# Softmax attention on one core: two maxima for one pass, by a Relu of key differences on ScalarE, and 64-row products in pairs

## The chip, the cores and the metric

The kernel runs on one core of one Trainium2 chip. The metric is the device time of one execution in microseconds; the runs of the kernel before have a median of 1805.18 us. The engines are named as in the profile: PE is TensorE, PEld its weight loads, DVE is VectorE, ACT is ScalarE, POOL is GpSimd, SP is the engine that issues most transfers.

## The reference

The kernel computes a small language-model tower: an embedding, a softmax attention, a layer of experts, a second attention with Relu features, and a second layer of experts. The change lies in the first attention and in the embedding stage that prepares it. Four sequences of 1024 tokens have 12 heads of 16 features each:

```python
qkv = jnp.einsum('bnhd,hde->bnhe', xh, W_qkv) + b_qkv
q, k, v = jnp.split(qkv, 3, axis=-1)
scores = jnp.einsum('bihd,bjhd->bhij', q, k) / scale
p = jax.nn.softmax(scores, axis=-1)
attn = jnp.einsum('bhij,bjhd->bihd', p, v)
```

## The kernel before, in words

**Parts and stacks.** Queries and keys are split into three bf16 parts (high, middle, low). A stack puts six products of parts above each other in 96 partitions (`Q_STACK`, `K_STACK`, lines 43 to 45), so that one bf16 matmul of 96 rows gives an almost exact f32 product. Row 96 of the query stack holds minus the maximum of each query, row 96 of the key stack ones, so that a matmul of 97 rows gives scores with the maximum taken off.

**Embedding** (`embed_and_project`, lines 161 to 373). Eight chunks of 512 tokens run through a two-deep pipeline. POOL gathers rows of the table three chunks ahead (line 211) and makes the low parts by three subtractions per chunk (line 217). SP waits for them (line 229) and sends the parts to memory in four transfers per chunk (line 235). ACT writes `full` and the high parts (lines 320, 321) after the sends of two chunks before (line 319); at the end it loads the stacks of batch 0, group 0 (line 331). The stage ends with all engines meeting (line 164 in the profile).

**Attention** (`softmax_attention`, lines 376 to 723). The heads stand in three groups of four (`NG`, `GH`). For each of four batches and three groups there are 16 steps (two halves of 512 queries, eight tiles of 128 keys). A step issues, in PE's order of line 694: scores of the next step for heads 0 and 1 (`scores`, line 647), one maximum product, scores for heads 2 and 3, two maximum products, the products of this step's probabilities with V (`times_v`, line 679), one more maximum product. ACT takes exponentials of two heads at a time (`exps`, line 610) out of four PSUM banks; PE waits for ACT before it writes these banks again (line 645).

**Maxima.** A group needs 64 maximum units: four heads, eight query tiles, two halves of the keys (`max_units`, line 426). PE writes a unit to one of three PSUM slots in turn (`produce`, lines 651 to 668), DVE reduces it (`consume`, line 553) and so frees the slot (`ring_free`). The units of the next group are made five steps ahead (`AHEAD`, line 430); before the loop, all 64 units of group 0 and 20 of group 1 are made alone (`before`, line 432). I call this the lead-in. At the end of a group DVE combines the halves (line 573), PE transposes the maxima, and SP sends them through memory into row 96 (`load_max`, lines 472 to 477). SP also loads each group's stacks for the next batch, in 12 transfers, once the group's scores are done (lines 502 to 505). The batch loop is a hardware loop over three batches, with the last batch written out behind it (`turns`, line 462).

Lines that the prediction names: 319 (ACT's wait for sends), 622 (ACT's copy of the output, once per eight steps).

## Time and profile before

| | us |
|---|---|
| median of 3 runs (lowest to highest) | 1805.18 (1803.73 to 1810.18) |
| the profiled execution's own time | 1795.51 |
| its span, first to last instruction | 1793.9 |
| embedding stage, to the meeting of the engines | 0 to 109 |
| lead-in, maxima only | 110 to 161 |
| loop of 192 steps | 161 to 732 |
| all later stages | 732 to 1794 |

The page gives the busy time of each engine in the span (PE 1596.3, DVE 1090.1, ACT 627.6, POOL 423.1 us), then the span in 40 slices of 44.8 us with a digit for each engine's busy tenths, then groups of instructions by line. Durations of PE's products include their way through the array, so products that follow each other overlap in the records; their pitch is read from start to start. An idle time in brackets belongs to the engine just before the instruction and names what ended it.

### The profile page before, as it was taken

To read this page: it belongs to the slowest core of one execution; us is meant where nothing else is said; L and a number is where in the kernel's file an instruction comes from. 1 tells how busy PE (TensorE), PEld (TensorE's weight loads), DVE (VectorE), ACT (ScalarE), POOL (GpSimd) and SP (SyncE) were. 2 spreads that over 40 slices of the span, in tenths; PEclk is the share of its full clock that TensorE was granted. 3 is DMA by queue.
4 is the path that set the end of the run, shared out by engine and by line. 5 is a ranking of instruction groups with operands and counts; after the bars stand their busy time and mean duration, and the time that the engine had idled before them with its cause. 6 is when DMAs were issued, how large, how long until landed. Compare 5 with 4: busy or idle time off the path is not lost. (4 is left out here: it accounts for less than half of the span.)

```text
span 1793.9 us, 28354 instructions
## 1 busy us (share of the span) xinstructions
PE 1596.3 (89%) x8964; PEld 865.2 (48%) x8965; DVE 1090.1 (61%) x2478; ACT 627.6 (35%) x849; POOL 423.1 (24%) x518
## 2 busy tenths in 40 slices
PE   4779999999899999875999947899988989999997
PEld 2422332233233332574566634567775656666664
DVE  5978997899799893356233335565544943333336
ACT  3412666576566668410211102222123112212111
POOL 6650000000000000100455525000000226666650
PEclk9866999999999999885899977999899889999999
DMA  2470222022222200630211112000001401111116
GB/s 78 151 169 1 37 37 36 1 35 35 36 35 36 36 1 1 154 119 16 60 42 39 39 46 64 1 10 19 10 18 51 126 18 51 53 50 53 46 42 216
DMA packets 64847, 92.82 MB, mean 52 GB/s; under 512 B 9905, under 2 KB 50036, under 8 KB 63732
## 3 DMA queue, kind: packets, MB, share of 16 engines
q1 hardware_dynamic: 51520, 65.08, 15.3%
q0 software_dynamic: 12288, 25.18, 4.9%
q10 hardware_dynamic: 960, 1.57, 0.4%
q8 instruction: 41, 0.67, 0.2%
q14 instruction: 38, 0.31, 0.1%
HBM read 61.82 MB, written 29.98 MB: 51 GB/s over the span
## 5 line engine op out<-in xcount | busy, mean ns | idle before, releaser
L553 DVE TENSOR_REDUCE sa_half_max<-psum 128x1 f32<-128x512 f32 x768 | 494.5, 687 | 68.8 <-PE psum L656 50.0
L610 ACT ACTIVATE sa_probs<-psum 128x1024 f32<-128x1024 f32 x384 | 372.3, 1022 | 167.2 <-PE psum L647 165.7
L656 PE MATMUL psum<-k_stack,q_stack 96*128 96x512 bf16 x768 | 285.5, 410 | 19.7 <-DVE sa_half_max L553 9.6
L647 PE MATMUL psum<-q_stack,k_stack 97*128 97x512 bf16 x768 | 231.1, 385 | 6.3 <-ACT sa_probs L610 5.4
L656 PEld LDWEIGHTS psum<-k_stack,q_stack 96*128 96x128 bf16 x768 | 75.0, 98 | 274.7 <-issue 133.2
L679 PE MATMUL psum<-sa_probs,sa_v_ext 128*32 128x512 f32 x1536 | 206.6, 610 | 0.6 <-ACT sa_probs L610 0.6
L1580 PE MATMUL psum<-w_e_up_a,ex_xt 128*128 x448 | 172.5, 528 | 0.0
L1430 ACT ACTIVATE ex_silu<-psum 128x384 f32<-128x384 f32 (+1 forms) x112 | 59.3, 529 | 290.8 <-PE psum L1580 288.3
L1470 DVE COPY ex_to_rows<-slot_rows 128x2 uint32 (+1 forms) x56 | 12.8, 229 | 211.5 <-DMA y_rows<-ex_y,ex_to_rows 117.4
L1596 PE MATMUL psum<-w_e_down,ex_g_t 128*128 x752 | 137.2, 334 | 0.5 <-DVE ex_g_t L1462 0.5
L1596 PEld LDWEIGHTS psum<-w_e_down,ex_g_t 128*128 128x128 f32 x752 | 120.7, 190 | 34.5 <-issue 34.5
L1364 POOL DMA_INDIRECT y_rows<-ex_y,ex_to_rows x112 | 110.7, 988 | 98.7 <-DVE ex_y L1471 70.5
L1455 DVE TENSOR_TENSOR ex_g<-ex_silu,psum 128x384 f32<-128x384 f32 (+1 forms) x112 | 67.0, 602 | 96.6 <-PE psum L1580 85.1
L1333 POOL DMA_INDIRECT ex_x<-x_tokens,ex_tokens x112 | 110.6, 988 | 55.6 <-POOL ex_tokens L1339 39.5
L542 POOL COPY sa_v_ext<-v_nat 128x512 f32 x12 | 7.2, 613 | 474.4 <-PE psum L679 474.0
L647 PEld LDWEIGHTS psum<-q_stack,k_stack 97*128 97x128 bf16 x768 | 72.7, 99 | 88.6 <-ACT sa_probs L610 28.8
L1580 PEld LDWEIGHTS psum<-w_e_up_a,ex_xt 128*128 128x128 f32 x448 | 84.3, 192 | 60.6 <-issue 32.1
L1573 PE MATMUL psum<-ex_w_b,ex_xt 64*128 64x384 f32 (+1 forms) x448 | 98.9, 560 | 6.5 <-ACT ex_xt L1424 3.2
L1108 POOL TENSOR_TENSOR sh_work<-sh_work 128x512 f32<-128x512 f32 x6 | 8.9, 1480 | 307.1 <-ACT sh_work L1167 305.3
L1424 ACT COPY ex_xt<-psum 128x512 f32<-128x512 f32 x56 | 32.8, 586 | 127.0 <-PE psum L1562 127.0
L1462 DVE COPY ex_g_t<-psum 128x384 f32<-128x384 f32 (+1 forms) x112 | 63.7, 605 | 15.1 <-PE psum L1587 12.6
L679 PEld LDWEIGHTS psum<-sa_probs,sa_v_ext 128*32 128x32 f32 x1536 | 30.3, 108 | 81.3 <-issue 75.1
(286 smaller groups left out, 2183.1 us busy)
## 6 DMA issues: line engine op xcount, KB each, us to landing
attn<-y_rows SPq DMA_DIRECT2D x24, 384.0 KB, 4.6
q_stack<-qk_parts SPq DMA_DIRECT2D x66, 128.0 KB, 4.3
k_stack<-qk_parts SPq DMA_DIRECT2D x66, 128.0 KB, 6.6
qk_parts<-qk_split SPq DMA_DIRECT2D x16, 384.0 KB, 3.5
x_tokens<-x SPq DMA_DIRECT2D x16, 384.0 KB, 2.6
qk_parts<-qk_split SPq DMA_DIRECT2D x16, 192.0 KB, 4.4
w_e_down<-e_down SPq DMA_DIRECT2D x1, 3072.0 KB, 32.6
out<-h SPq DMA_DIRECT2D x8, 384.0 KB, 4.0
```

Of the source, the lines that this page charges most:

```text
L553: nc.vector.tensor_reduce(half_max[:, g, hd, qt, half:half + 1], slot, AX.X, ALU.max).then_inc(ring_free[r], 1)
L610: nc.scalar.activation(probs[:, st % 2, 2 * pair:2 * pair + 2, :], ps[:, 2 * pair:2 * pair + 2, :], ACT.Exp, scale=SCALE0).then_inc(exp_do ...
L647: last = nc.tensor.matmul(ps[:, hd, :], kst[:, g, hd, kt * P:(kt + 1) * P], qst[:, g, hd, half * HALF:(half + 1) * HALF], start=True, stop ...
L656: last = nc.tensor.matmul(ps[:, 4 + r, :], qst[0:SK, g, hd, qt * P:(qt + 1) * P], kst[0:SK, g, hd, half * 512:(half + 1) * 512], start=Tru ...
L679: last = nc.tensor.matmul(ps[hd * W:(hd + 1) * W, OUT, :], v_ext[:, g, kt, hd, :], probs[:, st % 2, hd, :], start=(kt == 0), stop=(kt == T ...
L1333: pool.indirect_dma_start(out=x[:, u, :], out_offset=None, in_=x_tokens, in_offset=bass.IndirectOffsetOnAxis(ap=tokens[:, u:u + 1], axis=0 ...
L1364: pool.indirect_dma_start(out=y_rows, out_offset=bass.IndirectOffsetOnAxis(ap=to_rows[:, u:u + 1], axis=0), in_=y[:, u, :], in_offset=None ...
L1455: nc.vector.tensor_tensor(g[:, u, :], silu[:, u, :], ps[:, PS_UP + u, 0:F], ALU.mult).then_inc(g_done, 1)
L1462: nc.vector.tensor_copy(g_t[:, u, :], ps[:, PS_G + u, 0:F]).then_inc(g_t_done, 1)
L1573: last = nc.tensor.matmul(ps[:, bank + u, 0:F], xt[rows_of, u, v, :], w_b[rows_of, u, :], start=True, stop=False)
L1580: nc.tensor.matmul(ps[:, bank + u, 0:F], xt[:, u, v, :], w.up(u, v), start=False, stop=True).then_inc(done, 1)
L1596: last = nc.tensor.matmul(ps[:, PS_Y, u * D:(u + 1) * D], g_t[:, u, c * P:(c + 1) * P], w.down(u, c), start=(c == 0), stop=(c == FC - 1))
```

## The change

Each group of units in a step becomes: a difference product for an even head, a product of an odd head with the first half of the keys, a "both" product for the even head, a product of the odd head with the second half. The keys of an even head are taken in pairs (j and j + 256 of a chunk). The difference product gives q(near key) - q(far key); ACT writes its Relu to SBUF; the "both" product gives q(far key), and one DVE instruction adds the two and takes the maximum. All maximum products use only the first four parts, 64 rows: rows 0 to 63 for even heads, rows 64 to 127 for odd heads, whose stacks are laid out anew (four parts in rows 64 to 127, two in rows 0 to 31, the maximum in row 32, zeros up to row 63), so that their scores now use 128 rows. The differences of keys are made by POOL in the embedding stage and sent and loaded like the parts. The loads of batch 0, group 0 move from ACT's end to SP, between the sends.

```diff
+SENDS = 6
+MAX_ODD = SK - DB
+def max_rows_of(odd):
+    return slice(DB, P) if odd else slice(0, DB)
+def score_rows_of(odd):
+    return slice(0, P) if odd else slice(0, SK + 1)
+def load_stack(eng, s, b, g, which, odd):
+    stack, order = ((s.q_stack, Q_STACK), (s.k_stack, K_STACK))[which]
+    for k, part in enumerate(order):
+        row = (DB + k * HD) % P if odd else k * HD
...
+        eng.dma_start(stack[row:row + HD, g, odd::2, :], src[odd]).then_inc(s.loaded[g], 16)
+def load_differences(eng, s, b, g):
+    for k, part in enumerate(K_STACK[:DB // HD]):
...
+        eng.dma_start(s.d_stack[k * HD:(k + 1) * HD, g, :, :], src[0]).then_inc(s.loaded[g], 16)
+STACK_LOADS = 4 * len(Q_STACK) + DB // HD
@@ embed_and_project, POOL
+            def take_apart(u, k, link):
+                pool.wait_ge(two["sent"][u], START + 16 * SENDS * k)
+                near, far = full[:, u, 1:3, 0:CHUNK // 2], full[:, u, 1:3, CHUNK // 2:CHUNK]
+                high, middle = (differences[:, u, :, part, :] for part in range(2))
+                link(nc.gpsimd.tensor_tensor(apart[:], near, far, ALU.subtract))
+                link(nc.gpsimd.tensor_copy(high, apart[:]))
+                nc.gpsimd.tensor_tensor(middle, apart[:], high, ALU.subtract).then_inc(two["apart"][u], 1)
+                pool.wait_ge(two["apart"][u], START + k + 1)
...
+                if chunk >= 0:
+                    take_apart(u, k, Chain(pool, m["ep_apart_link"], 2, chunk))
@@ embed_and_project, SP
-            with sp.Fori(0, B) as b:
+            for b in range(B):
                 for u in range(2):
                     sp.wait_ge(two["low"][u], START + 3 * (b + 1))
+                    sp.wait_ge(two["apart"][u], START + b + 1)
...
+                    for r, (src, row) in enumerate(((slice(0, P), 0), (slice(DB, P), P))):
...
+                        sp.dma_start(dst.rearrange("c r t -> r c t"), differences[src, u, r]).then_inc(two["sent"][u], 16)
+                    early = 2 * b + u - 3
...
+                    if 0 <= early < 4:
+                        load_stack(sp, s, 0, 0, early // 2, early % 2)
+                    if early == 3:
+                        load_differences(sp, s, 0, 0)
@@ embed_and_project, ACT
-                    act.wait_ge(two["sent"][u], START + 64 * k)
+                    act.wait_ge(two["sent"][u], START + 16 * SENDS * k)
+                    act.wait_ge(two["apart"][u], START + k)
...
-                load_stacks(act, s, 0, 0)
@@ softmax_attention
         def max_units(g, first, last):
-            return [("max", g, k // (2 * TB), k // 2 % TB, k % 2) for k in range(first, last)]
+            units = []
+            for k in range(first, last):
+                odd, half, qt, hd = k % 2, k // 2 % 2, k // 4 % TB, k // (4 * TB) * 2
+                units.append(("max", g, hd + 1, qt, half) if odd else
+                             ("both" if half else "difference", g, hd, qt, half))
+            return units
@@ load_max
+            for odd, row in enumerate((SK, MAX_ODD)):
+                sp.dma_start(qst[row:row + 1, g, odd::2, :], rows[odd]).then_inc(max_loaded[g], 16)
@@ POOL
+            nc.gpsimd.memset(qst[MAX_ODD:DB, :, 1::2, :], 0.0).then_inc(v_init, 1)
+            nc.gpsimd.memset(kst[MAX_ODD:DB, :, 1::2, :], 0.0).then_inc(v_init, 1)
@@ DVE, consume
+                if kind == "difference":
+                    return
                 slot = ps[:, 4 + r, :]
                 dve.wait_ge(ring_full[r], START + k + 1)
+                if kind == "both":
+                    hd, qt, _ = unit[2:]
+                    r_near, k_near = near
+                    dve.wait_ge(ring_free[r_near], START + k_near + 1)
+                    dve.nop(nofuse=True)
+                    nc.vector.tensor_tensor_reduce(ahead_of[:, u], slot, ahead_of[:, u], 1.0, LOWEST, ALU.add, ALU.max,
+                                                   half_max[:, g, hd, qt, 0:1]).then_inc(ring_free[r], 1)
@@ ACT
+            def ahead(r, k, u, r_taken, k_taken):
+                act.wait_ge(ring_full[r], START + k + 1)
+                act.wait_ge(ring_free[r_taken], START + k_taken + 1)
+                nc.scalar.activation(ahead_of[:, u], ps[:, 4 + r, :], ACT.Relu).then_inc(ring_free[r], 1)
...
                         exps(b, g, st)
+                        for unit in step_units(g, st, last)[0]:
+                            if unit[0] == "difference":
+                                ahead_in_turn(b, place[last][unit], last)
@@ PE
-                    last = nc.tensor.matmul(ps[:, hd, :], kst[:, g, hd, kt * P:(kt + 1) * P],
-                                            qst[:, g, hd, half * HALF:(half + 1) * HALF], start=True, stop=True)
+                    rows = score_rows_of(hd % 2)
+                    last = nc.tensor.matmul(ps[:, hd, :], kst[rows, g, hd, kt * P:(kt + 1) * P],
+                                            qst[rows, g, hd, half * HALF:(half + 1) * HALF], start=True, stop=True)
...
+                if kind in ("difference", "both"):
+                    rows = max_rows_of(0)
+                    slot, keys = ps[:, 4 + r, :], s.d_stack[rows, g, hd // 2, :]
+                    if kind == "both":
...
+                    last = nc.tensor.matmul(slot, qst[rows, g, hd, qt * P:(qt + 1) * P], keys, start=True, stop=True)
...
-            ORDER = ("scores", "maxima", "scores", "maxima", "maxima", "outputs", "maxima")
+            ORDER = ("scores", "maxima", "scores", "maxima", "outputs")
...
+                                for unit in left[:2]:
+                                    produce(b, unit, *uses(b, n))
+                                    n += 1
+                                left = left[2:]
```

## Rows read from the trace of the kernel before

**Rows 1.** The page's slices: busy tenths of PE and DVE in 40 slices.

```profile
PE   4779999999899999875999947899988989999997
DVE  5978997899799893356233335565544943333336
```

**Rows 2.** Stretches: us, busy PE, PEld, DVE, ACT, POOL (count), clock, DMA, GB/s.

```profile
110.00:160.60 50.60, 49.08 (x86) 8.74 (x85) 49.67 (x85) 0.00 (x0) 16.93 (x18) 0.50 0.36 77
170.00:300.00 130.00, 129.61 (x742) 40.52 (x740) 119.43 (x198) 90.04 (x95) 1.23 (x2) 1.00 0.18 26
692.00:731.00 39.00, 37.77 (x224) 8.05 (x222) 1.84 (x6) 35.22 (x38) 0.00 (x0) 1.00 0.01 1
```

**Rows 3.** Timeline of one loop step: start, length in us, engine, line.

```profile
171.71 0.39 PE L656 MATMUL psum<-k_stack,q_stack 96*128 96x512 bf16 x1
...
171.93 0.60 PE L647 MATMUL psum<-q_stack,k_stack 97*128 97x512 bf16 x2
172.13 2.59 DVE L553 TENSOR_REDUCE sa_half_max<-psum 128x1 f32<-128x512 f32 x4 [0.24 <-PE psum L656]
...
172.65 1.94 ACT L610 ACTIVATE sa_probs<-psum 128x1024 f32<-128x1024 f32 x2 [0.90 <-PE psum L647]
...
173.02 0.60 PE L656 MATMUL psum<-k_stack,q_stack 96*128 96x512 bf16 x2
...
173.54 1.07 PE L679 MATMUL psum<-sa_probs,sa_v_ext 128*32 128x512 f32 x8
...
174.54 0.39 PE L656 MATMUL psum<-k_stack,q_stack 96*128 96x512 bf16 x1
```

**Rows 4.** Timeline of PE in the expert stage, 64-row products among full ones.

```profile
962.16 1.99 PE L1573 MATMUL psum<-ex_w_b,ex_xt 64*128 64x512 f32 x8
964.08 2.87 PE L1596 MATMUL psum<-w_e_down,ex_g_t 128*128 x16
966.78 3.60 PE L1580 MATMUL psum<-w_e_up_a,ex_xt 128*128 x8
970.22 0.60 PE L1562 MATMUL psum<-ident,ex_x 128*128 128x128 f32 x4
```

**Rows 5.** Line 622, all of its instructions: ns min/median/max, first and last start.

```profile
L622 ACT COPY sa_out_t<-psum x24: 586/586/592, 189.0 to 732.4; 128x512 f32<-128x512 f32 x24
```

**Rows 6.** Timeline where the batch loop jumps back.

```profile
306.77 1.28 ACT L610 ACT_TABLE_LOAD   x1
...
308.07 3.77 ACT L610 ACTIVATE sa_probs<-psum 128x1024 f32<-128x1024 f32 x4
309.15 0.61 PE L647 MATMUL psum<-q_stack,k_stack 97*128 97x512 bf16 x2 [1.62 <-ACT sa_probs L610]
...
316.03 2.48 DVE L553 TENSOR_REDUCE sa_half_max<-psum 128x1 f32<-128x512 f32 x4 [7.64 <-issue]
316.78 0.61 PE L656 MATMUL psum<-k_stack,q_stack 96*128 96x512 bf16 x1 [4.69 <-DVE sa_half_max L553]
```

**Rows 7.** DVE: the lead-in's first reductions, all reductions, and a product of two tensors.

```profile
110.17 15.03 DVE L553 TENSOR_REDUCE sa_half_max<-psum 128x1 f32<-128x512 f32 x25 [5.92 <-PE psum L656]
...
L553 DVE TENSOR_REDUCE sa_half_max<-psum x768: 670/691/697, 110.2 to 687.6; 128x1 f32<-128x512 f32 x192
...
L1455 DVE TENSOR_TENSOR ex_g<-ex_silu,psum 128x512 f32<-128x512 f32 x40 | 27.5, 688 | 51.9 <-PE psum L1580 48.7 <-ACT ex_silu L1430 1.9
```

**Rows 8.** POOL's subtractions around one chunk, and SP at the embedding's end.

```profile
64.45 1.15 POOL L217 TENSOR_TENSOR qk_split<-ep_rest,qk_split 128x512 bf16<-128x512 f32 x1 [0.36 <-DVE qk_split L268]
...
72.90 1.53 POOL L217 TENSOR_TENSOR qk_split<-ep_rest,qk_split 128x512 bf16<-128x512 f32 x1 [1.10 <-DVE qk_split L268]
74.79 1.15 POOL L217 TENSOR_TENSOR qk_split<-ep_rest,qk_split 128x512 bf16<-128x512 f32 x1 [0.36 <-DVE qk_split L268]
...
105.65 2.72 SPq L235 DMA_DIRECT2D qk_parts<-qk_split  x4
109.01 2.91 SPq L157 DMA_DIRECT2D q_stack<-qk_parts  x6
```

More of the change, by code:

```diff
@@ L236, in _ @@
                                      parts[src, u, min(r, 2), :, :]).then_inc(two["sent"][u], 16)
+                    cols = slice(u * (CHUNK // 2), (u + 1) * (CHUNK // 2))
+                    for r, (src, row) in enumerate(((slice(0, P), 0), (slice(DB, P), P))):
+                        n = src.stop - src.start
+                        dst = s.k_differences[:, b * D + row:b * D + row + n, cols]
+                        sp.dma_start(dst.rearrange("c r t -> r c t"), differences[src, u, r]).then_inc(two["sent"][u], 16)
+                    early = 2 * b + u - 3
+                    if early == 0:
+                        for w in range(2):
+                            sp.wait_ge(two["sent"][w], START + 16 * SENDS)
+                    if 0 <= early < 4:
+                        load_stack(sp, s, 0, 0, early // 2, early % 2)
+                    if early == 3:
+                        load_differences(sp, s, 0, 0)
         @block.vector
@@ L326, in step @@
                     copy_xt(*nxt)
-            def finish():
-                for u in range(2):
-                    act.wait_ge(two["sent"][u], START + 64)
-                load_stacks(act, s, 0, 0)
-            pipeline(act, B, start, step, finish)
+            pipeline(act, B, start, step, lambda: None)
         @block.tensor
@@ L460, in softmax_attention, with differences_of @@
         place = {last: {u: n for n, u in enumerate(order(last))} for last in (False, True)}
+        AHEAD_UNITS = [n for n, u in enumerate(before) if u[0] == "difference"]
+        def differences_of(last):
+            return [n for n, u in enumerate(order(last)) if u[0] == "difference"]
+        buffer_of = {last: {n: (len(AHEAD_UNITS) + i) % 2 for i, n in enumerate(differences_of(last))}
+                     for last in (False, True)}
+        PER_TURN = len(differences_of(False))
+        assert PER_TURN % 2 == 0
         def turns(eng, body):
@@ L514, in _ @@
             pool.wait_ge(v_init, START + 2)
-            nc.gpsimd.memset(kst[SK:SK + 1, :, :, :], 1.0).then_inc(ones_row, 1)
-            pool.wait_ge(ones_row, START + 1)
+            nc.gpsimd.memset(qst[MAX_ODD:DB, :, 1::2, :], 0.0).then_inc(v_init, 1)
+            nc.gpsimd.memset(kst[MAX_ODD:DB, :, 1::2, :], 0.0).then_inc(v_init, 1)
+            pool.wait_ge(v_init, START + 4)
+            for odd, row in enumerate((SK, MAX_ODD)):
+                nc.gpsimd.memset(kst[row:row + 1, :, odd::2, :], 1.0).then_inc(ones_row, 1)
+            pool.wait_ge(ones_row, START + 2)
             link = Chain(pool, constants)
@@ L578, in _ @@
                     combine(unit[1], lambda i: (i % SLOTS, i // SLOTS), n - 1)
-                consume(0, n, unit, n % SLOTS, n // SLOTS)
+                if unit[0] == "both":
+                    near = n - 2
+                    consume(0, n, unit, n % SLOTS, n // SLOTS, (near % SLOTS, near // SLOTS),
+                            AHEAD_UNITS.index(near) % 2)
+                else:
+                    consume(0, n, unit, n % SLOTS, n // SLOTS)
             def sequence(b, last):
@@ L593, in sequence @@
                         dve.wait_ge(max_stored[unit[1]], START + 16 * (b + 1 if unit[1] == 0 else b))
-                    consume(b, n, unit, r, k)
+                    if unit[0] == "both":
+                        near = place[last][("difference",) + unit[1:4] + (0,)]
+                        consume(b, n, unit, r, k, uses(b, near), buffer_of[last][near])
+                    else:
+                        consume(b, n, unit, r, k)
             turns(dve, sequence)
@@ L632, in sequence @@
                 copy_out(b, NG - 1, 1, last)
+            for i, n in enumerate(AHEAD_UNITS):
+                act.wait_ge(ring_full[n % SLOTS], START + n // SLOTS + 1)
+                if i >= 2:
+                    taken = AHEAD_UNITS[i - 2] + 2
+                    act.wait_ge(ring_free[taken % SLOTS], START + taken // SLOTS + 1)
+                nc.scalar.activation(ahead_of[:, i % 2], ps[:, 4 + n % SLOTS, :], ACT.Relu
+                                     ).then_inc(ring_free[n % SLOTS], 1)
             turns(act, sequence)
@@ L683, in _ @@
             for n, unit in enumerate(before):
-                if unit[0] == "max" and unit[2:] == (0, 0, 0):
+                if unit[0] == "difference" and unit[2:] == (0, 0, 0):
                     pe.wait_ge(loaded[unit[1]], START + 16 * LOADS)
```

80 lines of the change are left out of this document (48 added, 32 removed).

## The prediction

> **What bounds the kernel now.** I read the page's slices first [rows 1]: from the third slice to the fifteenth TensorE (PE) and VectorE (DVE) both stand at 7 to 9, and nothing says which one follows the other. So I cut the attention stage into stretches [rows 2]. In the lead-in, where the maxima of the first group are made, DVE is busy 49.67 of 50.60 us and PE runs at a granted clock of 0.50, the lower level (1.2 GHz): DVE sets the pace. In the loop (170 to 300 us) PE is busy 129.61 of 130 us at full clock, DVE 119.43, ScalarE (ACT) 90.04: PE sets it. In the last group, which has no maxima left to make, ACT and PE share it.
>
> One step of the loop shows PE's side [rows 3]. PE starts its first maximum product at 171.71 and the same product of the next step at 174.54: a step is 2.84 us (2.83 here). Two score products start at 171.93, 0.22 us after the product before them, which is the pitch. The last two maximum products start at 173.02. The products with V start at 173.54 and PE is back at 174.54, 1.00 us. DVE has four reductions in 2.59 us, ACT two exponentials in 1.94: both wait for PE.
>
> **The loop after the change.** A step now issues two scores, a pair of 64-row products (difference of an even head, first half of an odd one), two scores, a second pair (both, second half of the odd head), the products with V. All four maximum units still take turns over three PSUM slots, so the fourth unit takes the slot of the first, the difference. That slot is freed by the new Relu on ACT, no longer by DVE. This closes a circle through PE's in-order queue that did not exist:
>
> The two scores take two pitches, 0.44 us, then PE changes from 128 rows to 64. No such change is in the loop of before, but the expert stage has one [rows 4]: two pairs of 64-row f32 products take 962.16 to 964.08, 1.92 us, where four full products take 966.78 to 970.22, 3.44. Perfect pairs would be 1.72, so pairs do run side by side and entering and leaving cost 0.2 together, 0.1 each. The change into the 32-column shape before the V products agrees: 173.02 to 173.54 is 0.52 for two products, 0.09 more than two pitches [rows 3]. I take 0.09; the bounds are 0 and 0.11. From scores to difference: 0.53.
>
> The difference lasts as long as the other bf16 products, 0.39, and ACT starts 0.12 after a product's end (the two scores of 171.93 end at 172.53, the exponential starts at 172.65) [rows 3]: 0.51. The Relu reads 128x512 of PSUM and writes f32, as the copy of line 622 does in 0.59 [rows 5]. PE starts 0.06 after ACT ends: the first exponential of 308.07 ends at 309.09, the score waiting for it starts at 309.15 [rows 6]. So the fourth unit can start 0.51 + 0.59 + 0.06 = 1.16 us after the difference, while PE would be there after 0.85 (pair 0.22, change 0.09, scores 0.44, change 0.09). From it to the V products 0.22 + 0.09 = 0.31, and 1.00 back to the scores [rows 3].
>
> The circle is 0.53 + 1.16 + 0.31 + 1.00 = 3.00 us against 2.84: 0.16 more per step. Of the 768 maximum units [rows 7] 84 are made in the lead-in, the others in 684 / 4 = 171 steps: **+27 us**. Without any cost of changing shape the circle is 2.91 (+12); with the Relu's two waits (lines added in the function `ahead`) costing 0.05 more it is +36. The other engines stay inside 3.00: ACT 1.94 and about 0.5 for a queued Relu; DVE two reductions at 0.65 and one add with maximum. That one is not in the trace: its lower bound is the f32 add-like operation with a PSUM input, 0.69 [rows 7], its upper bound twice that, 1.38, and even this leaves DVE at 2.68. The steps without maxima are untouched.
>
> The Relu delays what stands behind it on ACT: the next step's exponentials start 0.5 us after it and the second one ends 2.9 us after the difference's start (0.51 + 0.5 + 1.94); PE asks for it at 3.3 (3.00 + 0.31). That is covered.
>
> **Lead-in.** No shape alternates here, and the Relu has the idle ACT to itself, so DVE goes on setting the pace. It has 84 reductions (64 of the first group, 20 of the second) at a pitch of 0.60 (25 in 15.03 us [rows 7]), 2.40 for four. After: two reductions and one add with maximum, 1.20 + 0.69 + 0.06 for its wait and no-op = 1.95. Of 21 such fours: **-9 us** (-12 if it costs no more than a reduction; +4 at 1.38).
>
> On the add with maximum the Trainium skill speaks too ("VectorE: DVE Perf Modes", section "Two Vector instructions with no wait between them"): an operation that also writes out its accumulator counts as two instructions. No run here shows it; by it, and a small DVE operation for the second, the term would be about -5 instead of -9.
>
> **Embedding.** POOL gets three operations of 512 elements per chunk; its only row of that size there takes 1.15, so 3.5 with their waits. In the chunks in which it also gathers, its last subtraction comes every 10.34 us (64.45 to 74.79), with 1.10 and 0.36 us of idle inside [rows 8]. 10.34 - 1.46 + 3.5 is 12.4, 2 us over the present rhythm. The first chunk and four more leave POOL 11.5 us behind, and line 319 makes ACT wait for the sends of two chunks before, which now follow POOL's work. At the end of the stage all engines meet, and SP comes last, after four sends of 0.68 each (2.72) [rows 8]; after the change it waits for 3.5 us more of POOL and issues two more sends. If later chunks without gathers win everything back, 4 us remain; if nothing, 16. Against it, group 0's stacks now arrive before the stage ends; but SP leaves the stage at 109.01 and the first reduction starts at 110.17 [rows 7, 8], product and all, so that is worth 0.5. I take **+11 us** (+3 to +16), in the middle.
>
> Other moves cost nothing where they lie. A group's stacks come in 28 loads instead of 12, on SP, at 0.48 each (six in 2.91 us [rows 8]) 13 us instead of 6, and are needed eleven steps (33 us) later; without that cover a group's maxima would wait for up to the 8 us more. One more load of a row of maxima is another 0.5 us with two steps to spare. Two zero fills are added on POOL, which is busy 16.93 of the 50.60 us of the lead-in [rows 2] and is needed only at its end; if they lasted longer than that idle time, the first V products would wait once.
>
> **Loop ends.** When the batch loop jumps back, DVE stands still for 7.64 us, and PE waits for it; ACT passes its own jump without idle, straight into a table load [rows 6]. DVE has some 213 operations in a pass, ACT 102; after the change ACT has 150, and the Relus' two waits each. By the rows alone ACT's jump costs between nothing and what DVE's does. Stopped from 306.8 to 314.4, ACT would end step 0's exponentials near 317.6 where PE now resumes with step 1 at 316.8: about one step, 3 us, twice: **+6 us** (0 to +14).
>
> The Trainium skill ("Runtime: NRT & Kernel Launch", section "Instruction fetch mechanics") has a rule that speaks against the change here: an engine's instruction memory is refilled in blocks of 256, and a jump out of the two blocks held must fetch first. The trace agrees for DVE (7.64 us); by it ACT's longer pass stalls too, and without it this term is 0.
>
> **Sum.** +27 - 9 + 11 + 6 = +35 us on the profiled execution's 1795.5: 1830.5. The runs shown have a median of 1805.18, 9.7 above that execution, so I state **1840 us**. All low ends together give 12 - 12 + 3 + 0 = +3, all high ends 36 + 4 + 16 + 14 = +70.
>
> **Rivals.**
> Faster: the slot comes back in time. The place is PE's wait before the second product of an odd head; it decides whether difference to freed slot takes more or less than 0.85 us. If less, PE alone sets the step: scores 0.88, pairs 0.44, V 0.86, five changes of shape 0.47, together 2.65 to 2.67. That saves 0.17 in 171 steps, 29 us; with -9, +11 and +4 the result is about 1782. For it speaks that ends of products are modelled; against it that the Relu alone is 0.59 and a product's visible latency 0.5. 0.12.
>
> No change: shapes cost nothing (the 0.09 belongs to the V products alone), POOL's work is won back, ACT does not stall: +12 - 9 + 4 + 0 = +7, 1812. The expert rows speak against the first half. 0.14.
>
> Not what it says: the pairs do not overlap because each product has its own wait. PE then needs 0.88 + 0.88 + 0.86 + 0.47 = 3.09, +43 in the loop, 1856. The expert pairs have no wait between them, so this is open. 0.08.
>
> Relu evicts the exponential's table: two loads of 1.28 [rows 6] in each step, 2200. The copy of line 622 stands between exponentials 24 times [rows 5], and the page's costliest groups show no load; this one follows a jump. 0.02. The add with maximum costs over 1.7: DVE sets a step of 3.2, 1880. 0.04.
>
> **Numbers.** The forecast keeps 0.60. This kernel's measurement can tell about 0.5%, 9 us. Faster: 0.12 and a little, 0.13. Same: most of the second rival and the low edge of the forecast, 0.15. Slower: 0.72. The range takes in the second and third rivals and leaves out the first, the table loads and the worst DVE case: 1803 to 1868.
>
> **What would show it.** In the loop: PE idle before the fourth unit, released by ACT's Relu, 0.3 us; step about 3.0; DVE down to 2.05 of it; clock 1.00. If PE starts the V products 1.2 us after the difference without such a wait, the circle is wrong. In the lead-in: 42 us at DVE's pace. In the embedding: POOL without idle while it gathers, SP's last sends near 119 us. At loop ends: ACT idle with nothing to wait for.

## The result and the profile after

The changed kernel takes 1828.51 us (median of 4 runs, 1825.27 to 1831.92), the kernel before 1806.28 (1803.73 to 1810.18): a ratio of 1.0121, 95% interval 1.0092 to 1.0151, so 17 to 27 us more. Its profiled execution took 1826.18 us, with a span of 1824.5 against 1793.9.

The page's slices, PE and DVE (to be read beside [rows 1]):

```profile
PE   4858999899899999876899965899988989999997
DVE  5968666566566665067333326556443853333336
```

PE still stands at 8 to 9 through the attention stage; DVE fell from 7 to 9 down to 5 to 6. The lead-in and a stretch of the loop (columns as in [rows 2]):

```profile
130.30:178.00 47.70, 38.76 (x89) 7.08 (x87) 42.37 (x87) 14.21 (x23) 27.61 (x21) 0.50 0.28 76
190.00:300.00 110.00, 107.55 (x585) 26.27 (x596) 75.21 (x158) 89.40 (x112) 1.23 (x2) 1.00 0.12 32
```

In the lead-in DVE is no longer full (42.37 of 47.70 us); in the loop PE still looks full (107.55 of 110), but that is the modelled end of its products, since the timeline of two steps has a wait in it:

```profile
184.13 0.39 PE L784 MATMUL psum<-d_stack,q_stack 64*128 64x512 bf16 x1
184.13 0.39 PE L788 MATMUL psum<-k_stack,q_stack 64*128 64x512 bf16 x1
...
184.55 0.60 ACT L716 ACTIVATE sa_ahead_of<-psum 128x512 f32<-128x512 f32 x1 [1.75 <-PE psum L784]
...
184.99 0.39 PE L784 MATMUL psum<-k_stack,q_stack 64*128 64x512 bf16 x1
...
185.21 0.39 PE L788 MATMUL psum<-k_stack,q_stack 64*128 64x512 bf16 x1
...
185.52 1.07 PE L811 MATMUL psum<-sa_probs,sa_v_ext 128*32 128x512 f32 x8
...
186.52 0.61 PE L770 MATMUL psum<-q_stack,k_stack 97*128 97x512 bf16 x2
...
187.06 0.39 PE L784 MATMUL psum<-d_stack,q_stack 64*128 64x512 bf16 x1
...
187.56 0.60 ACT L716 ACTIVATE sa_ahead_of<-psum 128x512 f32<-128x512 f32 x1 [0.58 <-PE psum L784]
...
187.92 0.39 PE L784 MATMUL psum<-k_stack,q_stack 64*128 64x512 bf16 x1
...
188.21 0.09 PEld L788 LDWEIGHTS psum<-k_stack,q_stack 64*128 64x128 bf16 x1 [0.20 <-ACT sa_ahead_of L716]
...
188.53 0.16 PEld L811 LDWEIGHTS psum<-sa_probs,sa_v_ext 128*32 128x32 f32 x8 [0.23 <-issue]
```

The first pair runs side by side: both products start at 184.13. The second does not: L788 comes 0.22 and 0.29 us behind L784, when the Relu has ended, and the row of 188.21 names it. From products with V to products with V it is 3.01 us (185.52 to 188.53); most other steps take 2.93. They differ in the Relu's start, 0.42 us after the difference (184.13 to 184.55) or 0.50 (187.06 to 187.56).

Stages can be compared in every profile by three starts, in us: the first maximum product, the first product with V and the last one (the kernels e1 to e12 are told of below).

| kernel | first maximum | first V | last V | span |
|---|---|---|---|---|
| before | 109.5 | 167.3 | 731.8 | 1793.9 |
| after | 129.7 | 181.7 | 761.7 | 1824.5 |
| e1 half a Relu | 128.0 | 180.3 | 725.8 | 1794.7 |
| e2 maxima first | 130.1 | 181.5 | 712.3 | 1780.2 |
| e3 differences on DVE | 132.3 | 184.3 | 765.6 | 1828.6 |
| e4 pairs only | 129.9 | 187.9 | 774.2 | 1838.1 |
| e5 no jumps | 131.3 | 181.9 | 747.1 | 1813.1 |
| e6 no differences made | 112.9 | 164.9 | 745.1 | 1809.0 |
| e7 before again | 112.5 | 170.3 | 735.3 | 1808.7 |
| e8 no write-out | 132.3 | 183.2 | 763.3 | 1830.7 |
| e9 before, loop moved | 111.9 | 169.7 | 719.4 | 1789.0 |
| e10 one part | 119.7 | 172.1 | 750.9 | 1817.0 |
| e11 three edits | 117.6 | 167.6 | 682.8 | 1745.9 |
| e12 pairs, maxima first | 112.0 | 167.5 | 684.9 | 1745.7 |

A kernel's time is 1.6 to 1.7 us more than its span. Of e1 to e12 only e2, e11 and e12 were run more than once, so the others are read by their stages. From the last product with V to the end, which no edit touches, it is 1060.8 to 1073.4 us in these rows. The first maximum product comes at 128.0 to 132.3 in the six kernels that share the embedding stage of after (after, e1, e2, e4, e5, e8), and at 109.5 and 112.5 in the two executions of the kernel before (e7 is one, see below).

After against before: embedding +20.2 us, lead-in 52.0 instead of 57.8, -5.8, the loop 580.0 instead of 564.5, +15.5, the rest +0.7. At the two jumps of the batch loop before, the two gaps between products with V (6.07 and 9.28 to 9.53 us) are 19.6 us longer in all than four steps of 2.84; after (9.58 to 9.68 and 3.71 to 3.76) 15.0 longer than four of 2.93. So the jumps got 4.6 us cheaper, and the steps with maxima cost 20.1 more, 0.12 each. (The step after each pair of gaps is longer too, 3.70 and 3.43 before, 3.01 after; counted as part of the jumps it makes them 5.9 cheaper and the steps 21.4 dearer.) The embedding's 20.2 is good to some 3 us only, by the spread just given.

### The profile page after: what moved, and what is told of

Same layout as the page of the kernel before. It is cut to its first block and busy times, and to the rows that moved or that the text cites. A ratio compares the mean times of both kernels' runs of the same rounds, so it can differ in the third digit from the quotient of the medians.

```text
span 1824.5 us, 29449 instructions
## 1 busy us (share of the span) xinstructions
PE 1609.6 (88%) x8907; PEld 839.2 (46%) x8965; DVE 992.6 (54%) x2481; ACT 722.6 (40%) x1041; POOL 458.7 (25%) x545
## 3 DMA queue, kind: packets, MB, share of 16 engines
q1 hardware_dynamic: 60488, 69.82, 13.3%
## 5 line engine op out<-in xcount | busy, mean ns | idle before, releaser
L643 DVE TENSOR_REDUCE sa_half_max<-psum 128x1 f32<-128x512 f32 x384 | 264.3, 688 | 119.3 <-PE psum L788 117.3
L770 PE MATMUL psum<-q_stack,k_stack 97*128 97x512 bf16 (+1 forms) x711 | 222.6, 390 | 12.1 <-ACT sa_probs L709 11.1
L788 PE MATMUL psum<-k_stack,q_stack 64*128 64x512 bf16 x384 | 158.9, 414 | 3.0 <-ACT sa_ahead_of L753 0.5
L639 DVE CUSTOM_DVE_ANT_0 sa_ahead_of<-psum,sa_ahead_of 128x512 f32<-128x512 f32 x192 | 132.7, 691 | 51.3 <-PE psum L784 50.3
L716 ACT ACTIVATE sa_ahead_of<-psum 128x512 f32<-128x512 f32 x171 | 102.1, 597 | 99.6 <-PE psum L784 93.2
L770 PEld LDWEIGHTS psum<-q_stack,k_stack 97*128 97x128 bf16 (+1 forms) x768 | 46.9, 98 | 195.2 <-ACT sa_probs L709 150.8
L1713 PEld LDWEIGHTS psum<-w_e_up_a,ex_xt 128*128 128x128 f32 x448 | 84.0, 191 | 60.3 <-issue 31.8
L784 PE MATMUL psum<-d_stack,q_stack 64*128 64x512 bf16 x192 | 79.4, 414 | 21.2 <-PEq L195 13.4
```

The lines of the kernel that those rows point to most:

```text
L639: nc.vector.tensor_tensor_reduce(ahead_of[:, u], slot, ahead_of[:, u], 1.0, LOWEST, ALU.add, ALU.max, half_max[:, g, hd, qt, 0:1]).then_in ...
L643: nc.vector.tensor_reduce(half_max[:, g, hd, qt, half:half + 1], slot, AX.X, ALU.max).then_inc(ring_free[r], 1)
L716: nc.scalar.activation(ahead_of[:, u], ps[:, 4 + r, :], ACT.Relu).then_inc(ring_free[r], 1)
L770: last = nc.tensor.matmul(ps[:, hd, :], kst[rows, g, hd, kt * P:(kt + 1) * P], qst[rows, g, hd, half * HALF:(half + 1) * HALF], start=True ...
L788: last = nc.tensor.matmul(ps[:, 4 + r, :], qst[rows, g, hd, qt * P:(qt + 1) * P], kst[rows, g, hd, half * 512:(half + 1) * 512], start=Tru ...
L1713: nc.tensor.matmul(ps[:, bank + u, 0:F], xt[:, u, v, :], w.up(u, v), start=False, stop=True).then_inc(done, 1)
```

## The experiments

**The slot: e1, e2, e4.** e1 shortens the Relu to half of the columns, here and in the lead-in:

```diff
-nc.scalar.activation(ahead_of[:, u], ps[:, 4 + r, :], ACT.Relu)
+nc.scalar.activation(ahead_of[:, u, 0:HALF // 2], ps[:, 4 + r, 0:HALF // 2], ACT.Relu)
...
```

> The Relu on ACT moves only the first 256 of the 512 columns of each difference; the other 256 are left out and stand at zero. Theory (the slot that the Relu frees is asked for too early): the Relu falls from 0.60 to about 0.38 us, the second product of the second pair starts beside the first one instead of 0.215 us behind it, and the loop's step falls from 2.93 or 3.01 to 2.72 us, which is what PE needs by itself (0.54 + 0.32 + 0.54 + 0.32 + 1.00). Over 171 steps some 40 us, near 1786. Rival (the second pair can't run side by side, because one of its products reads its keys in two pieces): the 0.215 us between its products stays, the step stays at 2.93, near 1826.

Timeline of PE and ACT in one step of e1:

```profile
207.39 0.39 PE L785 MATMUL psum<-d_stack,q_stack 64*128 64x512 bf16 x1 [0.15 <-issue]
...
207.82 0.38 ACT L717 ACTIVATE sa_ahead_of<-psum 128x256 f32<-128x256 f32 x1 [0.99 <-PE psum L785]
...
208.25 0.39 PE L785 MATMUL psum<-k_stack,q_stack 64*128 64x512 bf16 x1
208.26 0.39 PE L789 MATMUL psum<-k_stack,q_stack 64*128 64x512 bf16 x1
```

The Relu lasts 0.38 us, the second pair runs side by side, and plain steps take 2.72 us, or 2.79 where the Relu starts late. The loop is 545.5 us, 34.5 less. The pair can overlap; only the slot kept it from doing so.

e2 changes PE's order:

```diff
-ORDER = ("scores", "maxima", "scores", "maxima", "outputs")
+ORDER = ("maxima", "scores", "scores", "maxima", "outputs")
```

> Only PE's order in a step changes: pair, four scores, pair, products with V. Theory (slot asked for too early): from the difference to the fourth unit PE now needs 0.32 + 0.88 + 0.09 = 1.29 us, more than the 1.08 to 1.16 until the Relu has freed the slot, so the wait goes; one change of shape goes too, and the step is 2.57 to 2.62 us, some 62 us less over 171 steps, near 1765. Rival (PE's pairs and changes of shape, or ACT's queue, set the step): the scores now wait for exponentials that stand behind the Relu and the step stays at 2.85 to 3.0, 1810 to 1828.

One step of e2:

```profile
209.46 1.07 PE L811 MATMUL psum<-sa_probs,sa_v_ext 128*32 128x512 f32 x8
...
210.46 0.39 PE L784 MATMUL psum<-d_stack,q_stack 64*128 64x512 bf16 x1
...
210.78 1.04 PE L770 MATMUL psum<-q_stack,k_stack 97*128 97x512 bf16 x4
...
211.75 0.39 PE L784 MATMUL psum<-k_stack,q_stack 64*128 64x512 bf16 x1
211.76 0.39 PE L788 MATMUL psum<-k_stack,q_stack 64*128 64x512 bf16 x1
212.07 1.06 PE L811 MATMUL psum<-sa_probs,sa_v_ext 128*32 128x512 f32 x8
```

The step is 2.61 us (209.46 to 212.07), without a wait: 1.30 us lie between difference and fourth unit. 1782.3 us, ratio to the kernel before 0.9848 (0.9808 to 0.9888). The loop is 49 us shorter, not 62: the steps that also copy out take 3.22 and 3.40 us, where those of after take 3.41 to 3.49 and 3.14 to 3.22.

e4 keeps the order and makes every unit an ordinary maximum:

```diff
-units.append(("max", g, hd + 1, qt, half) if odd else
-             ("both" if half else "difference", g, hd, qt, half))
+units.append(("max", g, hd + odd, qt, half))
...
```

> The pairing alone: every unit is an ordinary maximum over 64 rows, with no difference, no Relu and no addition; the order on PE stays. Theory (not the Relu as such, but the slot of a step's first unit being asked for again 0.86 us later): the slot is now freed by a DVE reduction that starts 0.46 us after the product and lasts 0.69, so at 1.21 instead of 1.08 us, and the step gets longer, 3.06 us; the lead-in goes back to 2.40 us for four units. Near 1850. Rival (the Relu on ACT is the cost, and DVE's slot is in time as it was before): the step falls to 2.72, near 1795.

One step of e4, PE and DVE:

```profile
208.42 0.39 PE L786 MATMUL psum<-k_stack,q_stack 64*128 64x512 bf16 x2
...
208.84 2.48 DVE L641 TENSOR_REDUCE sa_half_max<-psum 128x1 f32<-128x512 f32 x4 [0.54 <-PE psum L786]
209.28 0.70 PE L786 MATMUL psum<-k_stack,q_stack 64*128 64x512 bf16 x2
```

The second pair, merged into one row, is 0.70 us long where the first is 0.39: its second product waits 0.31 for DVE. Plain steps all take 3.03 us. So it is not ACT or the Relu that costs, but the first unit's slot being asked for again 0.86 us later; a slot that DVE frees comes later still.

**The embedding stage: e3, e6, e10.** e3 moves the three operations from POOL to DVE, with the same operands:

```diff
-link(nc.gpsimd.tensor_tensor(apart[:], near, far, ALU.subtract))
+link(nc.vector.tensor_tensor(apart[:], near, far, ALU.subtract))
...
```

> The three operations that make the key differences in the embedding stage go from POOL to DVE; nothing else changes. Theory (POOL's added work sets the rhythm while it gathers, and holds up small DVE operations after that): POOL is as before, DVE has 1.8 us more per chunk in idle time it has anyway, and the first maximum product starts at 112 to 117 instead of 129.7 us; total near 1812. Rival (the two more sends and the longer chain of a chunk set the rhythm, wherever the work is done): it stays at 125 to 132 us, near 1826.

A miss: the first maximum product starts at 132.3, which is the rival's time; of the rival's two reasons e6 rules out the sends, and the longer chain of a chunk was not tested apart from DVE's load. The rows of e3 (first) and before for one stretch, columns as in [rows 2], show why; DVE had no idle time to give, 51.06 of 54 us are busy already before, and in e3 it gets through 117 operations where it had 138:

```profile
36.00:90.00 54.00, 35.63 (x116) 20.27 (x114) 50.23 (x117) 19.37 (x36) 32.42 (x28) 0.73 0.46 139
```

```profile
36.00:90.00 54.00, 41.38 (x162) 25.65 (x160) 51.06 (x138) 26.38 (x49) 35.08 (x31) 0.87 0.50 155
```

Over the whole stage DVE is busy 99.47 us in e3 and 77.69 before: 21.8 more, for a stage that is 22.8 longer.

e6 leaves POOL's operations out, and with them the waits of SP and ACT for them, and keeps the sends:

```diff
-                if chunk >= 0:
-                    take_apart(u, k, Chain(pool, m["ep_apart_link"], 2, chunk))
+                if chunk == -1:
+                    nc.gpsimd.memset(differences[:], 0.0).then_inc(m["ep_apart_link"], 1)
...
```

> POOL's three operations on the key differences are left out of the embedding stage (zeros are sent instead, so that the maxima of even heads are over their far keys and zero); the six sends, the early loads and everything else stay. Theory (POOL's operations cost twice: their own time while POOL gathers, and small DVE operations that last until POOL's operation ends, 2.1 us per chunk by the rows): chunks come every 10.0 to 10.4 us again and the first maximum product starts at 111 to 115 us instead of 129.7; total near 1811. Rival (the two more sends and the early loads on SP's queue hold up the chunks, since ACT waits for the sends of two chunks before): chunks stay at 11.5 to 12.4 us and the product at 122 to 130.

First maximum product at 112.9: POOL's operations, with the waits for them, cost 16.8 of the 20.2 us. The other 3.4 are within the spread: the kernel before stands at 112.5 in e7, and e12, which has neither these operations nor the sends, at 112.0. The way is to be seen in after, POOL's first added operation in two chunks, and a small DVE operation (128x4) beside another of POOL's operations:

```profile
47.27 1.26 POOL L243 TENSOR_TENSOR ep_apart<-ep_full 128x512 f32<-128x512 f32 x1
...
59.69 1.26 POOL L243 TENSOR_TENSOR ep_apart<-ep_full 128x512 f32<-128x512 f32 x1
...
99.70 1.21 POOL L245 TENSOR_TENSOR k_split<-ep_apart,k_split 128x512 bf16<-128x512 f32 x1
...
100.02 0.91 DVE L130 TENSOR_TENSOR ep_tmp<-ep_tmp,ep_var_eps 128x4 f32<-128x4 f32 x1
```

While POOL gathers, a chunk takes 12.42 us (47.27 to 59.69). And the DVE operation of 100.02 ends at 100.93, with POOL's (100.91). Two groups of DVE operations (busy us, mean ns of one) while POOL gathers, 36 to 96 us in after and 36 to 88 in e6:

```profile
L328 DVE CAST qk_split<-ep_rest 128x512 bf16<-128x512 f32 x15 | 17.7, 1183 | 0.5
...
L124 DVE TENSOR_SCALAR ep_var_eps<-ep_mv 128x4 f32<-128x4 f32 x5 | 4.6, 917 | 0.2
```

```profile
L318 DVE CAST qk_split<-ep_rest 128x512 bf16<-128x512 f32 x15 | 10.6, 705 | 0.5
...
L124 DVE TENSOR_SCALAR ep_var_eps<-ep_mv 128x4 f32<-128x4 f32 x6 | 1.0, 169 | 0.2
```

169 ns becomes 917, 705 becomes 1183. DVE's busy time hides this: an operation that is held up counts as busy. The Trainium skill ("SBUF — State Buffer", section "SBUF: two separate sides") says that some DVE operations and POOL's share a pair of ports that one of them holds for its whole instruction; the row of 100.02 agrees, since it ends when POOL's does.

These are two of the groups that grew. Over the whole stage they go from 457 to 731 ns and from 705 to 1028, while DVE's f32 subtractions fall from 855 to 702. All in all DVE is busy 80.90 us in e6 and 90.40 in after, 9.5 more, against 16.8 us of the stage.

e10 makes the difference in one part, with one POOL operation, and sends and loads no second part:

```diff
-link(nc.gpsimd.tensor_tensor(apart[:], near, far, ALU.subtract))
-link(nc.gpsimd.tensor_copy(high, apart[:]))
-nc.gpsimd.tensor_tensor(middle, apart[:], high, ALU.subtract).then_inc(two["apart"][u], 1)
+nc.gpsimd.tensor_tensor(differences[:, u, :, 0, :], near, far, ALU.subtract).then_inc(two["apart"][u], 1)
...
```

> The differences get one bf16 part instead of two: the second part is left out (zero), so that the maxima of even heads are a little off, which only moves the shift that scores and sums share. POOL does one subtraction per chunk instead of three operations. Theory (POOL's operations cost the embedding stage, by their own time and by DVE operations that last until POOL's end): a chunk costs POOL 10.34 - 1.46 + 1.2 = 10.1 us and keeps its rhythm of 10.3; the first maximum product starts at 113 to 117 us instead of 129.7; the rest as in the changed kernel, near 1812. Rival (one operation holds DVE up as three do): 122 to 130.

In between, 119.7, outside both expectations. POOL in e10:

```profile
46.59 1.26 POOL L244 TENSOR_TENSOR k_split<-ep_full 128x512 bf16<-128x512 f32 x1
...
56.95 1.15 POOL L259 TENSOR_TENSOR qk_split<-ep_rest,qk_split 128x512 bf16<-128x512 f32 x1 [1.10 <-DVE qk_split L329]
58.06 1.26 POOL L244 TENSOR_TENSOR k_split<-ep_full 128x512 bf16<-128x512 f32 x1
```

A chunk takes 11.47 us (46.59 to 58.06), the old 10.34 and the added operation's pitch. POOL's idle 1.10 us, which I had subtracted, is still there: POOL waits for DVE, and DVE moves with POOL.

**The jumps: e5, e7, e9.** e5 writes the loop out on two engines:

```diff
-            with eng.Fori(0, B - 1) as b:
-                body(b, False)
+            if eng in (nc.vector, nc.scalar):
+                for b in range(B - 1):
+                    body(b, False)
+            else:
+                with eng.Fori(0, B - 1) as b:
+                    body(b, False)
```

> The batch loop of the attention stage is written out four times on DVE and ACT instead of jumping back; all else is as in the changed kernel. Theory (at the two jumps ACT stands for 2.8 us and DVE for 3.0 because instructions are fetched after a jump, and in the loop every third step or so the Relu waits 0.08 us longer for a register operation between its two waits): the two gaps of 9.6 + 3.7 us between products with V fall to about 4.6 + 2.9, as at the third batch end, which has no jump, 5.6 us each; the steps of 3.01 become 2.93, some 4 us more; together 15 us, near 1810. Rival (straight code is fetched no faster than after a jump, or the gap comes from copying out and the table load): the gaps stay and the total stays at 1820 to 1828.

Where the loop jumps back, after:

```profile
330.24 1.28 ACT L709 ACT_TABLE_LOAD   x1 [2.47 <-issue]
...
332.62 1.04 PE L770 MATMUL psum<-q_stack,k_stack 97*128 97x512 bf16 x2 [4.07 <-ACT sa_probs L709]
...
334.26 0.69 DVE L643 TENSOR_REDUCE sa_half_max<-psum 128x1 f32<-128x512 f32 x1 [4.86 <-PE psum L788]
```

and the same place in e5:

```profile
327.32 1.95 ACT L713 ACTIVATE sa_probs<-psum 128x1024 f32<-128x1024 f32 x2
...
328.40 0.61 PE L774 MATMUL psum<-q_stack,k_stack 97*128 97x512 bf16 x2 [0.21 <-ACT sa_probs L713]
```

ACT's idle 2.47 us and the table load behind it are gone, and PE waits 0.21 instead of 4.07. All plain steps take 2.93, so the 0.08 of every second or third one went with the loop's registers; in after, too, it is gone in the last batch, which is written out there. The loop is 565.2 us, 14.8 less, as expected.

e7 put 64 no-ops on DVE ahead of the loop.

> The kernel before, with 64 no-ops on DVE at the end of the embedding stage, where DVE waits for the other engines: they only move what follows to other places in DVE's instruction stream. Theory (how long DVE stands at a jump is decided by where the loop's first instructions lie, not by how many the loop has: 7.8 and 8.0 us here, 2.9 with a longer loop in the changed kernel): the stall at both jumps changes to 0.3 to 3 us, and the time falls by 5 to 10 us against a profiled execution of the kernel before. Rival (the length of the loop, 305 instructions, or the traffic at that time sets the stall): it stays at 7.8 us.

None of the no-ops is in the trace (DVE has as many instructions as before), so this is the kernel before a second time and tells nothing on either theory. It shows how far two executions lie apart: its span is 14.8 us longer, 3.5 of it by the last product with V and 11.3 in stages behind, which the change does not touch.

e9 uses instructions that do appear in the trace:

```diff
...
+            def finish():
+                for i in range(48):
+                    nc.vector.memset(pad[:, i:i + 1], 0.0)
-            pipeline(dve, B, start, step, lambda: None)
+            pipeline(dve, B, start, step, finish)
```

> The kernel before, with 48 one-element fills on DVE at the end of the embedding stage, where DVE waits some 6 us for the other engines: they move DVE's later instructions by 48 places. Theory (where the loop's first instructions lie decides how long DVE stands at a jump): the stalls of 7.8 and 8.0 us change to 0.3 to 3 us, and the gaps of 6.07 + 9.3 us between products with V shrink by 4 to 7 us each. Rival (the length of the loop or the traffic of that moment decides): 7.8 us stays.

DVE around the jump in e9, to be read beside [rows 6]:

```profile
310.31 0.42 DVE L568 TENSOR_TENSOR attn<-psum,sa_inv 128x256 f32 x1
...
312.35 0.69 DVE L557 TENSOR_REDUCE sa_half_max<-psum 128x1 f32<-128x512 f32 x1 [1.62 <-PE psum L660]
```

The 7.64 us without a cause are gone: DVE waits 1.62 us, for a product. The loop takes 549.7 us instead of 564.5. The same instructions, 48 places further on, are worth 14.8 us. A shift in time is not what does it: in e7 the loop starts 3.0 us later than before and takes 565.0. From 306 to 316 us the queue that carries instructions (q14) moves two packets in the kernel before and none in e9, so the stop goes with a fetch of instructions.

Two of the runs above settle what the jumps do in after. ACT at the jump in e4, which has no Relus:

```profile
336.13 1.28 ACT L707 ACT_TABLE_LOAD   x1
```

ACT passes without the idle 2.47 us, as it does before; so its stop came with the Relus. Whether it is the length of ACT's pass or the place of its code that decides, no run separates. And in e3, with other code ahead of DVE's loop, DVE goes from its branch (332.0) to its next instruction in 0.3 us, where in after it takes 3.0 (329.1 to 332.1). Yet the two gaps between products with V stay: 13.5 and 13.4 us in e3, 13.3 and 13.4 in after. So in after it is ACT's stop that sets them, and not DVE's.

**The lead-in: e8.** The addition with maximum becomes a plain one, and zero stands for its maxima:

```diff
-nc.vector.tensor_tensor_reduce(ahead_of[:, u], slot, ahead_of[:, u], 1.0, LOWEST, ALU.add, ALU.max,
-                               half_max[:, g, hd, qt, 0:1]).then_inc(ring_free[r], 1)
+nc.vector.tensor_tensor(ahead_of[:, u], slot, ahead_of[:, u], ALU.add).then_inc(ring_free[r], 1)
...
```

> DVE's addition with maximum becomes a plain addition with the same operands: the maximum that it writes out is left out (zero stands for the maxima of even heads). Theory (the write-out of the accumulator is an instruction of its own that costs DVE some 0.18 us, beside 0.615 for the addition and 0.135 for its wait): four units of the lead-in take 1.96 us instead of 2.14, some 4 us in 21 fours; the loop's step stays at 2.93 or 3.01, because it is not DVE's. Near 1821. Rival (the addition itself is slower than the product of two tensors that it was priced by): 2.14 stays.

Four units in after and in e8:

```profile
146.06 0.69 DVE L639 CUSTOM_DVE_ANT_0 sa_ahead_of<-psum,sa_ahead_of 128x512 f32<-128x512 f32 x1
...
146.67 0.08 DVE L639 DVE_READ_ACCUMULATOR2_ANT sa_half_max<- 128x1 f32 x1
146.67 1.48 DVE L643 TENSOR_REDUCE sa_half_max<-psum 128x1 f32<-128x512 f32 x2
...
146.82 0.61 PE L788 MATMUL psum<-k_stack,q_stack 64*128 64x512 bf16 x1
...
148.20 0.69 DVE L639 CUSTOM_DVE_ANT_0 sa_ahead_of<-psum,sa_ahead_of 128x512 f32<-128x512 f32 x1
```

```profile
146.12 0.69 DVE L639 TENSOR_TENSOR sa_ahead_of<-psum,sa_ahead_of 128x512 f32<-128x512 f32 x1
...
146.73 1.47 DVE L642 TENSOR_REDUCE sa_half_max<-psum 128x1 f32<-128x512 f32 x2
...
148.21 0.69 DVE L639 TENSOR_TENSOR sa_ahead_of<-psum,sa_ahead_of 128x512 f32<-128x512 f32 x1
```

2.14 becomes 2.09, not 1.96: the theory misses, and the rival's 2.14 is nearer without being met. The write-out is a row of its own (0.08) but worth 0.05, 1 us in the lead-in. What stays is two reductions in 1.48 (in e11's loop two back to back take 1.29): the second one's product (146.82) only starts when the addition has freed its slot (146.67 + 0.08 + 0.06), and lasts 0.61 at this clock (granted 0.50). The 0.19 between 1.48 and 1.29 is what four units take beyond the forecast (2.14 against 1.95). So here too the turn of the three slots sets the pace, DVE's operations among its steps, and not DVE by itself.

**Together: e11, e12.** e11 is e2, e5 and e10 in one. e12 is e4 with e2's order and e5's loop, and with the making, sending and loading of differences taken out.

> Three edits together: maxima first in a step, differences with one part (second part left out), and the batch loop written out on DVE and ACT. Theory (the three costs are separate and in series): the last products with V start at 761.3 - 49.5 (order, by the run of it alone) - 15 (embedding) - 13 (no jumps) = 684 us instead of 761.3, and the total is 1746 to 1760. Rival (one of the gains was only there because another cost hid behind it, as DVE's jump behind ACT's): 1765 to 1782.

> The pairing alone, with maxima first and the loop written out on DVE and ACT: no differences are made, sent or loaded, and all maxima are DVE reductions. Theory (once the order is right PE sets the step, and DVE's four reductions of 0.62 to 0.65 just fit): the step is 2.62 as with the differences, the lead-in is back at 2.40 us for four units (5 us more), the embedding at 110 to 112; total 1748 to 1762, the same as with differences within the measurement. Rival (DVE becomes the bound without the differences): steps of 2.7 to 2.8, 10 to 30 us more than the kernel with all three edits.

e11: 1753.08 us, ratio 0.9699 (0.9679 to 0.9720). e12: 1748.65 us, ratio 0.9689 (0.9664 to 0.9714). Both beat both kernels; between them there is no difference to be told. Both take 2.62 us for a step. 200 to 300 us in e11, then e12 (columns as in [rows 2]):

```profile
200.00:300.00 100.00, 97.40 (x589) 25.98 (x592) 73.43 (x162) 90.06 (x113) 1.85 (x3) 1.00 0.15 42
```

```profile
200.00:300.00 100.00, 97.68 (x587) 26.37 (x590) 95.29 (x161) 70.80 (x76) 1.84 (x3) 1.00 0.14 40
```

The differences take DVE from 95.29 to 73.43 us and put the Relus on ACT (70.80 to 90.06), but PE sets the step in both. With the right order they bring next to nothing in the loop (515.2 us against 517.4), and a shorter lead-in (50.0 us against 55.5) for a longer embedding stage (117.6 against 112.0).

## Why the prediction was right

Slower was right, and 1828.5 lies in the range, 11.5 below the stated time. The sum of +35 stands against +30.6 between the two profiled executions and +22 between the medians; e7 shows that one execution of the kernel before can lie 15 above another, mostly outside this stage. Of the 11.5, the sum makes only 4.3; the rest comes from the 9.7 that were added because the profiled execution of the kernel before was a quick one, while that of after lies 2.3 below its median. That the sum is so close is luck: the embedding was 9 too low and the loop ends 11 too high, and these two errors cancelled.

- **The loop, +27.** Right in mechanism: steps of 3.01 as forecast (3.00), PE's wait before the fourth unit, released by the Relu. e1 took the wait away in most steps by a shorter Relu, e2 altogether by another order, and e4, where DVE frees the slot, made it 0.1 us longer. Size: +20, because in most steps the Relu starts 0.42 us after the difference, not 0.51. The changes of shape cost what the rows of the expert stage gave, 0.1 each: scores to difference is 0.54, 0.53 forecast.
- **The lead-in, -9.** Measured -5.8. The step that failed is "DVE goes on setting the pace": DVE's second reduction waits 0.19 us in every four units for a product that waits for a slot. The rule of the Trainium skill ("VectorE: DVE Perf Modes", "Two Vector instructions with no wait between them"), that an operation which also writes out its accumulator is two instructions, had given -5 as the alternative. The second instruction is there in the rows, but e8 shows that it is worth 1 us and not the difference; that -5 came close is luck too. (The prediction's upper end for this term, with an addition of 1.38, comes to +5, not +4, which changes nothing.)
- **The embedding stage, +11.** Measured +20.2, beyond the range's +16. POOL's chunk of 12.4 us came as forecast (12.42), and ACT waits for sends as forecast (1.75 us before 71.07 and 2.47 before 84.30, for `k_differences`). What failed is "in the middle" between winning everything back later and nothing: later chunks also got longer (ACT's first writes for the fifth and the eighth chunk lie 37.0 us apart in after, 31.8 before and 34.1 in e7). DVE, which I had left out of this term, was busy 51 of 54 us and is held up by POOL's operations. The formula was luck as well: e10 shows that POOL's idle time can't be subtracted.
- **The loop ends, +6.** Measured -4.6. ACT does stand now, as forecast, and e4 shows that this came with the Relus; but it stands for 2.47 us and not for DVE's 7.64, by which the term was sized. The Trainium skill ("Runtime: NRT & Kernel Launch", "Instruction fetch mechanics") says that a jump to a place outside the two blocks held waits for a fetch; the packets of q14 agree with it, and no run here shows how large the blocks are. What failed besides is that DVE's 7.64 us would stay: with other code ahead of the loop DVE's stop is 3.0 us and over before PE, which waits for ACT, goes on. e9 shows for the kernel before, and e3 for this one, that the code ahead of the loop decides DVE's stop.
- **At nothing.** The 28 loads, the two loads of maxima and POOL's fills stayed hidden: in the waits of PE from 176 to 762 us none is for a stack, one of 0.3 us is for a row of maxima, and what follows the stage changed by 0.7 us.

Of the rivals, the slot that comes back in time is what e1 makes true: 2.72 us a step, where I had 2.65 to 2.67. That pairs do not overlap is refuted by the rows of 184.13. Table loads between Relu and exponential do not occur: there are three in the whole stage, as before. No change, with shapes at no cost, is refuted by the 0.54 us from scores to difference, and an addition of over 1.7 us by the rows of 146.06 (0.69 and 0.08).

What stays open: how the embedding stage's 16.8 us divide between POOL's own rhythm and DVE being held up (its busy time grew by 9.5). The lower granted clock there (0.70 in after from 36 to 90 us, 0.87 before) is not what makes it long: at nearly the same clock the first maximum product comes at 112.0 in e12 (0.79) and at 128.0 in e1 (0.81). No run gives the kernel before the new order, so what the order is worth without the 64-row pairs is not shown.

## What to carry to other kernels

When work moves to a faster form, look at who frees the buffer that the next product wants, and how soon it is asked for again: the order of issue was worth more here (49 us) than the operations saved, and with the right order the cleverer half of the change, the differences (in e11 with one part), was worth nothing that could be measured. Before giving POOL more work beside a busy DVE, look for DVE operations whose time grows when POOL works, and add up all of DVE's time, since others may shrink. Before reading a gain or loss into a loop's end, move the loop's code by some instructions: it may be worth 15 us by itself.

## What the runs showed of the hardware

- A 64-row pair starts two products within 0.01 us; each change between 128 and 64 rows costs 0.1 us (0.54 for two score products of 0.22 and a change).
- The stop at a jump depends on where the code lies: 7.64 us of idle DVE became 1.62 of waiting for a product when 48 small instructions were put ahead of the loop (e9), and 3.0 us from a branch to the next instruction became 0.3 with other code ahead (after, e3).
- A DVE operation on 128x4 elements (the `ep_var_eps` one) takes 0.17 us in the mean without POOL's added operations and 0.92 beside them, while POOL gathers.
- An addition with maximum of 128x512 is two rows, 0.69 and 0.08 us.
- In a loop with a register for its count, a Relu with two waits starts 0.08 us later in every second or third step; written out, it does not.
